# Four transformer layers on one core: maxima's rows turned later, and the fourth layer's bias of the maxima added by VectorE

## The reference, cut to what matters

```python
x = x + L0_attn(xn) + L0_ffn(xn)   # 16 heads of 8, causal softmax; 16 experts, top 4
x = x + L1_attn(xn) + L1_ffn(xn)   # 8 heads of 64, decayed linear attention; 8 experts, top 1
x = x + L2_attn(xn) + L2_ffn(xn)   # 16 heads of 8, causal softmax; adapter with the least rebuild loss
x = x + L3_attn(xn) + L3_ffn(xn)   # 16 heads of 8, full softmax with bias by distance; top 2 experts
# L3_attn
energy = einsum('bhqd,bhkd->bhqk', q, k)
rel = clip(pos[:, None] - pos[None, :] + (N - 1), 0, 248)
att = softmax((energy + bias_table[rel].T) / (sqrt(128) * temp), axis=-1)
```

## Time and profile before

| | |
|---|---|
| Median of 3 runs | 2943.17 us (2936.72 to 2946.89) |
| The profiled execution's own time | 2933.07 us |
| Its span | 2931.2 us |
| PE busy | 2476.0 us (84%) |
| DVE busy | 1543.2 us (53%) |
| ACT busy | 1325.9 us (45%) |
| POOL busy | 589.7 us (20%) |
| Granted TensorE clock | 0.947 of full, mean |

### The profile page before, as it was taken

How to read it: one execution, slowest core, us unless ns; L and a number is a source line. 1 busy time by engine, 2 the same in 40 slices (tenths; PEclk the granted TensorE clock), 3 DMA queues, 4 the chain that set the end, 5 groups by cost and what they waited for, 6 DMA issues and landing times. The chain is left out here.

```text
span 2931.2 us, 46008 instructions
## 1 busy us (share of the span) xinstructions
PE 2476.0 (84%) x16332; PEld 1580.8 (54%) x16466; DVE 1543.2 (53%) x3816; ACT 1325.9 (45%) x2462; POOL 589.7 (20%) x594
## 2 busy tenths in 40 slices
PE   3888887888884999999694788888877999999997
PEld 2455554787872666667693344444444555555553
DVE  6777775000013555654334666666636666666652
ACT  0455555444433333231131355555542666666665
POOL 3534331000006555441003111111001000000000
PEclk9999999999996899999896799999988999999999
DMA  3222221666661000000462211111112011111111
GB/s 113 90 87 73 78 85 43 185 196 190 199 179 57 23 25 26 19 19 4 127 187 79 71 44 52 54 53 49 46 42 66 28 44 50 50 50 41 32 34 30
DMA packets 117395, 214.10 MB, mean 73 GB/s; under 512 B 21000, under 2 KB 90160, under 8 KB 110256
## 3 DMA queue, kind: packets, MB, share of 16 engines
q1 hardware_dynamic: 104048, 186.88, 21.3%
q0 software_dynamic: 10240, 20.99, 2.5%
q10 hardware_dynamic: 2880, 3.28, 0.4%
HBM read 158.50 MB, written 51.40 MB: 72 GB/s over the span
## 5 line engine op out<-in xcount | busy, mean ns | idle before, releaser
L535 DVE TENSOR_REDUCE arena<-bank 128x1 f32<-128x512 f32 (+3 forms) x1216 | 775.7, 658 | 494.5 <-PE bank L525 246.7
L601 ACT ACTIVATE arena<-bank 128x512 f32<-128x512 f32 x640 | 373.3, 599 | 352.2 <-PE bank L591 347.6
L511 PE MATMUL bank<-arena 125*128 125x512 bf16 (+3 forms) x1536 | 460.2, 335 | 38.2 <-DMA arena<-q_parts 26.0
L601 ACT ACTIVATE arena<-bank,arena 128x512 f32<-128x512 f32 x512 | 337.3, 688 | 232.1 <-PE bank L586 73.0
L579 PE MATMUL bank<-arena 128*128 128x512 bf16 (+3 forms) x1402 | 389.2, 322 | 19.4 <-ACT arena L601 12.1
L616 PE MATMUL bank<-arena 128*32 128x512 f32 (+3 forms) x3072 | 315.8, 499 | 0.9 <-ACT arena L601 0.8
L579 PEld LDWEIGHTS bank<-arena 128*128 128x128 bf16 x1536 | 136.9, 99 | 248.6 <-ACT arena L601 140.1
L926 POOL DMA_INDIRECT back_rows<-sorted_out,back_now x160 | 154.3, 964 | 534.1 <-issue 256.2
L511 PEld LDWEIGHTS bank<-arena 125*128 125x128 bf16 x1536 | 139.7, 99 | 159.7 <-DVE arena L535 61.5
L1160 ACT ACTIVATE arena<-bank,arena 128x256 f32<-128x256 f32 x320 | 132.0, 470 | 195.4 <-PE bank L1210 195.4
L1306 DVE TENSOR_TENSOR arena<-bank,arena 128x256 f32<-128x256 f32 x80 | 33.9, 424 | 336.1 <-PE bank L1006 336.1
(11 more groups left out here) (250 smaller groups left out, 3709.5 us busy)
## 6 DMA issues: line engine op xcount, KB each, us to landing
arena<-in_L_ffn_w SPq DMA_DIRECT2D x80, 578.0 KB, 4.0
arena<-k_parts SPq DMA_DIRECT2D x48, 576.0 KB
arena<-q_parts SPq DMA_DIRECT2D x48, 576.0 KB
arena<-in_L_ffn_w SPq DMA_DIRECT2D x24, 768.0 KB, 4.6
arena<-sorted_in SPq DMA_DIRECT2D x104, 128.0 KB, 2.4
sorted_out<-arena SPq DMA_DIRECT2D x104, 128.0 KB, 4.0
k_parts<-arena SPq DMA_DIRECT2D x24, 384.0 KB
q_parts<-arena SPq DMA_DIRECT2D x72, 128.0 KB
```

Source lines behind the costliest of these rows:

```text
L511: ins = pe.matmul(mx[:, k * w:(k + 1) * w], Qx[0:KMAX, h, q * P:(q + 1) * P], Kx[0:KMAX, h, 0:w], start=(k == 0 or not L.causal), stop=not ...
L535: dve.reduce_max(L.mx[:, g % 2, q, heads[0]:heads[-1] + 1], mx[:, 0:w * len(heads)].rearrange("p (j k) -> p j k", k=w), AX.X).then_inc(L.m ...
L601: act.activation(L.probs[:, n % L.PR, 0:w], st[:, 0:w], ACT.Exp, scale=L.scale).then_inc(L.st_free.sem, 1)
```

## The change

1. Softmax layers: max_rows, copy_rows and send_rows 1.2 slots later (3.2, 3.8 and 4.1 after the point 8 slots before the group, in place of 2.0, 2.6 and 2.9); turn and divide 1.0 slot later, and turn_att, copy_att, out, add_out 1.0 to 1.2 later.
2. Third layer: rebuild steps 1.9 slots apart in place of 1.6, starting 1.0 earlier; a and copy_a 2.0 later.
3. Fourth layer: the fp32 matmuls that add the bias to the maxima's scores are removed. DVE reduces the columns without bias, and for the others adds the bias (transposed, from a new SBUF tile `tilt`) and takes the maximum in one tensor_tensor_reduce; one more small operation joins both maxima. At the layer's start eight more rounds of four transposes and a copy make `tilt`.
4. Fourth layer: center to choose 9.5 slots sooner; the second hidden step next to the first and in bank 0; the ring of probabilities holds 8 in place of 16.

```diff
@@ pe_max
-                far = L.biased and q < 2
                 ins = pe.matmul(mx[:, k * w:(k + 1) * w], Qx[0:KMAX, h, q * P:(q + 1) * P],
-                                Kx[0:KMAX, h, 0:w], start=(k == 0 or not L.causal), stop=not (L.causal or far),
+                                Kx[0:KMAX, h, 0:w], start=(k == 0 or not L.causal), stop=not L.causal,
                                 skip_group_check=L.causal)
-                if far and q == 0:
-                    pe.matmul(mx[:, 2 * P:3 * P], L.bias[:, h, P:2 * P], ident[:],
-                              start=False, stop=False)
-                    ins = pe.matmul(mx[:, 3 * P:4 * P], L.bias[:, h, 0:P], ident[:],
-                                    start=False, stop=True)
-                if far and q == 1:
-                    ins = pe.matmul(mx[:, 3 * P:4 * P], L.bias[:, h, P:2 * P], ident[:],
-                                    start=False, stop=True)
@@ dve_max
-            dve.reduce_max(L.mx[:, g % 2, q, heads[0]:heads[-1] + 1],
-                           mx[:, 0:w * len(heads)].rearrange("p (j k) -> p j k", k=w),
-                           AX.X).then_inc(L.mx_free.sem, 1)
+            far = (2 - q) * P if L.biased and q < 2 else 0
+            ins = dve.reduce_max(L.mx[:, g % 2, q, heads[0]:heads[-1] + 1],
+                                 mx[:, 0:w * len(heads) - far].rearrange("p (j k) -> p j k", k=w - far), AX.X)
+            if far:
+                j = heads[0]
+                dve.wait_ge(L.mx_free.sem, L.mx_free.at(START, n))
+                settle(dve)
+                ins = dve.tensor_tensor_reduce(
+                    out=L.shifted[:, 0:far], in0=mx[:, w - far:w], in1=L.tilt[:, g * HG + j, 0:far], scale=1.0,
+                    scalar=LOWEST, op0=ALU.add, op1=ALU.max, accum_out=L.mx_far[:, g % 2, q, j:j + 1])
+            ins.then_inc(L.mx_free.sem, 1)
...
+            if L.biased:
+                link(dve, L, dve.tensor_tensor(m[:, 0:2, :], m[:, 0:2, :], L.mx_far[:, g % 2], ALU.max))
@@ lay_out
-                    steps += [(begin - LAST_MAX + 2.0, "max_rows", g, 0, b),
-                              (begin - LAST_MAX + 2.6, "copy_rows", g, 0, b),
-                              (begin - LAST_MAX + 2.9, "send_rows", g, 0, b),
-                              (end + 2.2, "attended", g, 0, b), (end + 4.6, "turn", g, 0, b),
-                              (end + 5.4, "divide", g, 0, b)]
+                    steps += [(begin - LAST_MAX + 3.2, "max_rows", g, 0, b),
+                              (begin - LAST_MAX + 3.8, "copy_rows", g, 0, b),
+                              (begin - LAST_MAX + 4.1, "send_rows", g, 0, b),
+                              (end + 2.2, "attended", g, 0, b), (end + 5.6, "turn", g, 0, b),
+                              (end + 6.4, "divide", g, 0, b)]
@@ layer0 own
-                    (47.2, "turn_att", 0), (47.9, "copy_att", 0), (49.2, "out", 0), (50.0, "add_out", 0)]
+                    (48.2, "turn_att", 0), (48.9, "copy_att", 0), (50.2, "out", 0), (51.0, "add_out", 0)]
@@ layer2 own
-                        (-30.0 + 1.6 * e, "rebuild", e), (-29.4 + 1.6 * e, "differ", e), (-28.5 + 1.6 * e, "square", e))] + [
-                    (-15.5, "loss", 0), (-14.6, "choose", 0),
-                    (37.0, "a", 0), (37.7, "copy_a", 0),
-                    (47.2, "turn_att", 0), (47.9, "copy_att", 0), (49.2, "out", 0), (50.2, "add_out", 0)]
+                        (-31.0 + 1.9 * e, "rebuild", e), (-30.3 + 1.9 * e, "differ", e), (-29.4 + 1.9 * e, "square", e))] + [
+                    (-15.2, "loss", 0), (-14.4, "choose", 0),
+                    (39.0, "a", 0), (39.7, "copy_a", 0),
+                    (48.2, "turn_att", 0), (48.9, "copy_att", 0), (50.4, "out", 0), (51.4, "add_out", 0)]
@@ layer3
-            L = attention_plan(3, False, ["xnT", "k", "q", "v", "merit"],
-                               ["pt0", "pt1", "h0", "h1", "pt2", "pt3", "mix", "aT", "out"],
-                               [bank[3], bank[4], bank[7]], [bank[5], bank[6]], 16, None, True, copies=NHALF)
+            L = attention_plan(3, False, ["xnT", "k", "q", "v", "merit", "h1"],
+                               ["pt0", "pt1", "h0", "pt2", "pt3", "mix", "aT", "out"],
+                               [bank[3], bank[4], bank[7]], [bank[5], bank[6]], 8, None, True, copies=NHALF)
...
-                    (-60.0, "center", 0), (-57.0, "scale", 0), (-55.0, "norm", 0), (-54.3, "copy_norm", 0),
-                    (-53.0, "k", 0), (-52.2, "split_k", 0), (-50.4, "split_k_rest", 0),
-                    (-51.0, "q", 0), (-50.3, "split_q", 0), (-48.5, "v", 0), (-47.7, "add_v", 0),
-                    (-46.5, "choice", 0), (-45.7, "choose", 0),
-                    (39.0, "hidden", 0), (39.7, "gelu", 0), (43.8, "hidden", 1), (44.5, "gelu", 1),
+                    (-69.5, "center", 0), (-66.5, "scale", 0), (-64.5, "norm", 0), (-63.8, "copy_norm", 0),
+                    (-62.5, "k", 0), (-61.7, "split_k", 0), (-59.9, "split_k_rest", 0),
+                    (-60.5, "q", 0), (-59.8, "split_q", 0), (-58.0, "v", 0), (-57.2, "add_v", 0),
+                    (-56.0, "choice", 0), (-55.2, "choose", 0),
+                    (40.2, "hidden", 0), (40.3, "hidden", 1), (41.2, "gelu", 0), (41.3, "gelu", 1),
                     (67.2, "mix", 0), (68.2, "add_mix", 0),
-                    (71.2, "turn_att", 0), (71.9, "copy_att", 0), (73.0, "out", 0), (73.8, "add_out", 0)]
+                    (72.2, "turn_att", 0), (72.9, "copy_att", 0), (74.0, "out", 0), (74.8, "add_out", 0)]
@@ layer3 pe bias
+                    for n in range(H // 2, H):
+                        pe.wait_ge(L.bias_free, n + 1 - len(rounds))
+                        for c in range(4):
+                            h, block = 2 * (n - H // 2) + c // 2, slice(P, 2 * P) if c % 2 == 0 else slice(0, P)
+                            ins = pe.transpose(rounds[n % len(rounds)][:, c * P:(c + 1) * P], L.bias[:, h, block],
+                                               ident[:])
+                        ins.then_inc(L.bias_full, 1)
```

More of the change, by code:

```diff
@@ L24 @@
 KMAX = P - NPART
+LOWEST = float(np.finfo(np.float32).min)
 LN_EPS = 1e-05
@@ L179, in build @@
                 for n, e, k in ((0, E0, TOP0), (1, E1, 1))}
-        ARENA = 41344
+        ARENA = 41600
         arena = sb("arena", [P, ARENA])
@@ L2066, in layer3 @@
             L.bias = carve([P, H, HANKEL])
+            L.tilt = carve([P, H, HANKEL])
+            L.shifted = carve([P, HANKEL])
+            L.mx_far = carve([P, 2, 2, HG])
             L.hankel = L.probs[:, 0:H * HANKEL // T, :].rearrange("p a (c i) -> p (a c) i", i=HANKEL)
@@ L2092, in own @@
             def own(n):
-                start = [(-54.0, "loaded", 0), (-30.0, "bias", 0)] if n == 0 else []
+                start = [(-63.5, "loaded", 0), (-30.0, "bias", 0)] if n == 0 else []
                 return start + [
-                    (-60.0, "center", 0), (-57.0, "scale", 0), (-55.0, "norm", 0), (-54.3, "copy_norm", 0),
-                    (-53.0, "k", 0), (-52.2, "split_k", 0), (-50.4, "split_k_rest", 0),
-                    (-51.0, "q", 0), (-50.3, "split_q", 0), (-48.5, "v", 0), (-47.7, "add_v", 0),
-                    (-46.5, "choice", 0), (-45.7, "choose", 0),
-                    (39.0, "hidden", 0), (39.7, "gelu", 0), (43.8, "hidden", 1), (44.5, "gelu", 1),
+                    (-69.5, "center", 0), (-66.5, "scale", 0), (-64.5, "norm", 0), (-63.8, "copy_norm", 0),
[3 more added lines that the diff above has]
+                    (40.2, "hidden", 0), (40.3, "hidden", 1), (41.2, "gelu", 0), (41.3, "gelu", 1),
                     (67.2, "mix", 0), (68.2, "add_mix", 0),
-                    (71.2, "turn_att", 0), (71.9, "copy_att", 0), (73.0, "out", 0), (73.8, "add_out", 0)]
+                    (72.2, "turn_att", 0), (72.9, "copy_att", 0), (74.0, "out", 0), (74.8, "add_out", 0)]
             lay_out(L, own)
@@ L2195, in bias @@
                                   start=True, stop=True).then_inc(L.bias_full, 1)
-                    pe.wait_ge(L.bias_free, H // 2)
+                    for n in range(H // 2, H):
[5 more added lines that the diff above has]
+                        ins.then_inc(L.bias_full, 1)
+                    pe.wait_ge(L.bias_free, H)
                 def choice(pe, L, b, _):
@@ L2250, in bias @@
                 def bias(dve, L, b, _):
-                    for n in range(H // 2):
+                    for n in range(H):
+                        dst, m = (L.bias, n) if n < H // 2 else (L.tilt, n - H // 2)
                         dve.wait_ge(L.bias_full, n + 1)
-                        dve.tensor_copy(L.bias[:, 2 * n:2 * n + 2, :].rearrange("p h i -> p (h i)"),
+                        dve.tensor_copy(dst[:, 2 * m:2 * m + 2, :].rearrange("p h i -> p (h i)"),
                                         rounds[n % len(rounds)][:]).then_inc(L.bias_free, 1)
```

## The result

The changed kernel takes 2960.78 us (median of 5 runs, 2960.41 to 2966.99); the kernel before took 2943.17 beside it. The ratio is 1.0076, with a 95% interval of 1.0052 to 1.0100: slower by 0.8%, little but clear of the noise, where 2843 and "faster" were forecast. Measured once more beside the kernel before, it was 1.0049 (1.0012 to 1.0085). The profiled execution took 2965.29 us, with a span of 2963.5.

A forecast was written before the change was run, and what follows sets the result against it. PE was taken to bound all three softmax layers. Fourth layer -70, first -9 and third -21 made -100 us from the profiled 2933.07, so 2833, or 2843 for the median; own range 2820 to 2868, wider range 2800 to 2892.

The forecast's parts named there:

- Fourth layer, steps moved 9.5 sooner: Fourth layer: center to choose earlier lets SP's expansion follow the pick sooner, keeping the order safe; nothing gained, nothing lost.
- Bias matmuls -84: Fourth layer: PE sheds three 0.22 us matmuls a head, 10.6 us a batch, 84 us in all, taken whole.
- rival 1: Stalls change places: PE meets DVE and ACT, half of the 84 us left, sum -32, 2911 us; chance 0.16.
- Rows' DMA +14: Fourth layer: maxima's rows sent later, so the score waits 2.3 us once a batch, 0.3 of it before; +14 us.
- gelus adjacent -5: Fourth layer: gelu next to gelu saves 2 of 4 table loads of 1.28 us a batch on ACT; -5 us.
- DVE +8: Fourth layer: DVE's added bias work stays hidden, but its longer step is charged 1 us a batch, +8 us.
- Rival 3: Slow tensor_tensor_reduce, 1.6 us each, makes DVE bound the fourth layer; 3017 us, deciding from 1.3 us; chance 0.05.
- the wider spacing of the rebuilds: Third layer: rebuild steps further apart were to remove 4 of 6.7 us of PE's waits; -4 us.
- my 60%: Share of PE's waits before L558 that later rows remove: -23 us in the first layer, -22 in the third.
- The signs: Expected: fourth-layer batches 75 to 79 us, PE above 88%, L558 waits under 15 us each, rows' DMA waits 40 us.
- Rival 2: The rows' DMA is not hurt and all 75 us of waits go: at most -160, about 2803 us; chance 0.10.
- rival 4: DVE still waits for the same banks and PE's freed time becomes idle, within 0.3% (9 us); chance 0.03.

## Why the prediction was wrong

**The step that failed.** It is "Fourth layer, steps moved 9.5 sooner ... Nothing gained, nothing lost". I followed what SP does after the splits, and the rows that I used for it already held the answer: the pick is issued at the out step, slot 10 of a batch. `choose` was moved to slot 64 - 55.2 = 8.8. It waits for the experts picked before to have landed, so after the change it stands 1.2 slots ahead of the step that sets off what it waits for. Before, `choose` stood at slot 18.3 and the out step at 9, so there were 9 slots to spare. I had listed DVE, ACT and PE as doing "the same work for these steps", and looked up no wait of theirs. The cost is 60 us in the changed kernel, shown by putting two steps back. Doing that part alone on the kernel before costs 41. (The slot 22.7 in the same passage is 21.9 by its own rows, slot 9 and 17.3 us at 1.34 a slot; nothing hangs on it.)

**The sum of the fourth layer without it.** Forecast -70, measured 716.5 - 752.8 = -36. By terms:
- Bias matmuls -84. In a batch PE is busy 9.3 us less with the bias on DVE, forecast 10.6. Over the layer PE's busy time fell by 65 us with the bias alone (663.6 to 598.5), and to 599.6 in the best kernel. The distance of the starts was read rightly, to take it whole for the layer was not.
- What I put at nothing: the idle time that comes back. With the bias alone it was 36 us, so that 29 were left of the 84. PE's waits for the exponentials rose from 10.4 us to 27.3 there, and to 16.8 with `choose` put back. This is rival 1, stalls that change places, though in the changed kernel the wait stays well under the 30 us that I had named as its sign. It held beside the failed step, where I gave it 0.16 in place of it.
- Rows' DMA +14. With `choose` put back the wait is 18.6 us, 2.1 before: +16.5, so rightly sized in its place. But its price is more than the wait. Removing the waits gave 28 us: these 18.6, and 5.6 to 10.5 us less of PE's busy time (610.1 to 604.6 and 599.6 in the two runs), as the clock falls after a wait (below).
- gelus adjacent -5: the wait for the exponentials fell from 27.3 to 16.8 us between the bias alone and `choose` put back, twice the forecast, but other steps moved too, so this term is not shown by itself. `turn` later -3: the wait before L630 (L632 after) went from 5.7 us to 0.9.
- DVE +8: 5 measured. The size of DVE's work was wrong, and rightly called hidden. I took mean durations as time occupied, +4.9 to +11.0 us a batch. By durations it would be 16 x (419 + 556 + 415 + 281 + 2 x 83 - 1372) = 7.4 us; but the operations overlap, and DVE's busy time rose by only 2.0 us in a batch (54.2 to 56.2, the bias alone) and 20 us in the layer (439.3 to 459.1). The timeline has the next pair start 0.66 us after the first, for durations of 0.40, 0.41 and 0.08:

```profile
2441.17 0.40 DVE L528 TENSOR_REDUCE arena<-bank 128x1 f32<-128x256 f32 x1
2441.49 0.41 DVE L534 CUSTOM_DVE_ANT_0 arena<-bank,arena 128x256 f32<-128x256 f32 x1
...
2441.83 0.42 DVE L528 TENSOR_REDUCE arena<-bank 128x1 f32<-128x256 f32 x1
```

- That the operation shows as a main part and a read agrees with what I drew from the Trainium skill (VectorE: DVE Perf Modes, section Two Vector instructions with no wait between them); the read takes 83 ns, between my bounds of 0 and 190. Rival 3 is refuted: 415 ns where it needed 1300.
- More rounds at the start: 0, right; PE waits for the expanded rows 7.4 us in place of 12.3, so the cover shrank and held.

**The third layer.** Forecast -21, measured +10.7. Of this the wider spacing of the rebuilds costs 20 (628.5 to 608.7), where I had -4. I read the 6.7 us of waits at L1984 as something that spacing would end, and did not follow the last rebuild to `loss`, which has half the distance. Without it the layer gains 6.3 us (608.7), as much as by the rows alone (608.7 as well): the later `a` removed its wait for divide (7.8 us, L1995), and the -7 that I gave it did not come. The rows took away 33 us of waits where I had 22; the waits of L511, those for the DMA and the lower clock gave most of it back.

**The first layer.** Forecast -9, measured -7.5. The waits before L558 went from 38.2 us to 3.6, more than my 60%, and those for the rows' DMA from 2.3 to 20.8, +18.5 for the +14:

```profile
PE bank L581 <- DMA arena<-arena: 20.8, 9, 3.4
...
PE bank L560 <- DVE arena L549: 3.6, 8, 0.6
```

**The signs.** A batch of the fourth layer took 92.6 us for 75 to 79, with PE busy for 81% of it for above 88%. The waits before the rows fell under 15 us each, as said. Those for the rows' DMA came to 64.8 us in the three layers, where 40 were named.

**Rival 2**, that the rows' DMA would not be hurt, is refuted in all three layers (20.8, 19.2 and 24.8 us of waits); rival 4 as well. Rival 2's sum was also wrong: from the 45 us that I counted to all of the 75 are 30, not 20.

**The best kernel** is the changed one with `choose` and the rebuilds put back, Q expanded by three DMAs in the third and fourth layer, and the fourth layer's expansion held until the third group's rows are through: 0.9559 and 0.9563 of the kernel before on a chip where that takes 3024 us. Of the 134 us that it gains there, 64 are the fourth layer's and 31 the third's by the lengths above; most of the rest must lie in the first layer (565.0 us), whose length before was not profiled on that chip. On the chip with 2943 us it was not run; from 2884.24 - 28 (fourth layer) - 17 to 24 (third layer) I estimate 2832 to 2839 us there.

## What to carry to other kernels

When a step is moved in a written order, list for each of its instructions, on every engine, the semaphores that it waits for, and the place in the same order of what sets them: a step that is moved past the trigger of its own wait stops its engine once in every iteration, with little to see of it in the engines' busy times. Matmuls taken off a full engine count in full only until the next engine or DMA is met; here 39% was left in a batch (3.6 of 9.3 us). And a small DMA that is needed soon is best kept out of the time of a bulk one: making the bulk one wider gained 17 to 23 us in one layer and lost 24 in the other, and wider together with starting it between two small ones gained 28 in the second.

## What the hardware showed that I had not expected

**Half clock after a wait.** After a wait of 3 us for the rows' DMA, L511 and L581 start 0.43 us apart, where the same two start 0.22 apart 4 us earlier (2466.00 and 2466.22), and the granted clock of the next stretch is 0.57 of full speed, so that part of it runs at 1.2 GHz and not 2.4. Around the wait of 8.69 us it is 0.81. First the timeline of PE, then the two stretches by window:

```profile
2466.00 0.38 PE L511 MATMUL bank<-arena 125*128 125x512 bf16 x1
2466.22 0.38 PE L581 MATMUL bank<-arena 128*128 128x512 bf16 x1
...
2470.22 0.61 PE L581 MATMUL bank<-arena 128*128 128x512 bf16 x1 [2.97 <-DMA arena<-arena]
2470.62 0.63 PE L511 MATMUL bank<-arena 125*128 125x512 bf16 x1
2471.05 0.63 PE L581 MATMUL bank<-arena 128*128 128x512 bf16 x1
```
```profile
2433.00:2451.00 18.00, 8.28 (x41) 4.45 (x39) 6.00 (x24) 4.67 (x7) 2.72 (x4) 0.81 0.42 115
2470.00:2474.00 4.00, 3.78 (x13) 0.75 (x14) 1.46 (x4) 1.37 (x2) 0.00 (x0) 0.57 0.02 8
```

A PE that runs at half the clock also counts as busy for longer: of the same instructions PE is busy for 623.1 us in the changed kernel's fourth layer, at a mean clock of 0.90, and for 599.6 and 604.6 in the best kernel's two runs, at 0.95 and 0.94. So I estimate that 19 to 23 us of the layer's 777 are the waits' after-effect, in no list of waits.

**A small DMA beside a large one.** The 12 KB of the rows take 6 to 7 us while the expansion with Q in one DMA is in flight (5.97 and 6.80 us in the changed kernel, 6.84 before), 12.4 us when the expansion runs at 0.68, to its end, and at most 2.3 us when none is in flight.

**The first layer differs between chips.** The same order of the rows takes 513.3 us on one chip and 609.5 and 613.8 on another, and there the later rows gain 31 to 48 us in it in place of 7.5 (578.1 and 566.3). A third chip takes 564 to 569 with the later rows. In the third and fourth layers the chips differ no more than runs on one chip do (615.0, 616.6 and 617.4; 628.0 and 628.5; 716.6 and 716.5). No run was made for it, but the traces show what the stops look like: with the rows alone moved, PE, ACT and DVE all stand from 93 to 107 us of the span, while POOL issues indirect DMAs until 104, and the profile names as ACT's releaser only `remote` (44.3 us in the first layer, 13 times, longest 16.8). In the kernel before on the chip with 2943 us ACT has no such wait. What lies behind it stays open.
